# Attention inside a four-block transformer kernel: a shorter lead of the score tiles, and v copied and biased elsewhere

## The reference, cut to what matters

```python
# attention 0 (causal; H = 16 heads of 16)
q, k, v = x @ Wq[h] + bq[h], x @ Wk[h] + bk[h], x @ Wv[h] + bv[h]
probs = softmax(q @ k.T * 16**-0.5 + causal)       # 1024 x 1024 for each head
y = concat_heads(probs @ v) @ Wo + bo
# attention 1: no biases, no mask, q and k turned by rotary tables
```

## Time and profile before

| | |
|---|---|
| median of 3 runs | 689.41 us (688.97 to 691.52) |
| the profiled execution | 690.84 us, its span 689.1 us |
| PE, DVE, ACT, POOL busy | 590.9, 519.1, 349.9, 168.9 us |
| mean granted TensorE clock | 0.901 of 2.4 GHz |
| attention 0: first transposed piece, last row of exponentials | 44.95, 166.17 us |
| attention 1: first transposed piece, last row of exponentials | 370.57, 540.02 us |

### The profile page before, as it was taken

One profiled execution on the slowest core, in us unless ns is written; L12 is line 12 of the kernel. 1 busy time (PEld: TensorE's weight loads), 2 busy tenths in 40 slices (PEclk: granted clock), 3 DMA queues, 4 the chain that ended last, 5 costly groups with the idle time before them and its releaser, 6 DMA issues. The chain is left out here.

```text
span 689.1 us, 12664 instructions
## 1 busy us (share of the span) xinstructions
PE 590.9 (86%) x4702; PEld 406.7 (59%) x4702; DVE 519.1 (75%) x1041; ACT 349.9 (51%) x670; POOL 168.9 (25%) x280
## 2 busy tenths in 40 slices
PE   3989999988489999966979999999999756988793
PEld 2745555545368888855844444444444544778793
DVE  4788888975647777775768899999995587798536
ACT  3226777763145333331223788888888424154451
POOL 4234555563013222130500011111111000014520
PEclk9959999998779999997975999999999955899997
DMA  4534555622231111001340244344332225033431
GB/s 163 67 87 68 88 84 86 93 60 47 54 114 47 46 46 46 23 2 61 42 51 2 39 64 62 50 68 58 55 58 62 50 95 177 1 135 99 150 77 61
DMA packets 27541, 47.15 MB, mean 68 GB/s; under 512 B 13232, under 2 KB 18464, under 8 KB 26208
## 3 DMA queue, kind: packets, MB, share of 16 engines
q1 hardware_dynamic: 22112, 39.11, 27.9%
q0 software_dynamic: 4288, 7.20, 3.8%
q10 hardware_dynamic: 1088, 0.13, 0.1%
HBM read 25.22 MB, written 7.83 MB: 48 GB/s over the span
## 5 line engine op out<-in xcount | busy, mean ns | idle before, releaser
L467 ACT ACTIVATE probs<-ps 128x512 f32<-128x512 f32 x448 | 213.3, 562 | 82.7 <-PE ps L384 82.2
L360 PE MATMUL ps<-k_stack,q_stack 62*128 62x512 f32 x448 | 175.0, 468 | 7.4 <-DVE row_max L563 3.3
L384 PE MATMUL ps<-q_stack,k_stack 64*128 64x512 f32 x448 | 161.8, 439 | 9.6 <-ACT probs L467 5.9
L563 DVE TENSOR_REDUCE row_max<-ps 128x1 f32<-128x1024 f32 x128 | 149.8, 1215 | 17.3 <-PE ps L360 17.3
L384 PEld LDWEIGHTS ps<-q_stack,k_stack 64*128 64x128 f32 x448 | 77.2, 192 | 82.9 <-ACT probs L467 64.1
L399 PE MATMUL ps<-probs,v_ones 128*32 128x256 f32 (+7 forms) x2048 | 118.9, 350 | 4.3 <-POOL probs L518 3.6
L360 PEld LDWEIGHTS ps<-k_stack,q_stack 62*128 62x128 f32 x448 | 80.3, 200 | 37.6 <-DVE row_max L563 16.5
L560 DVE CUSTOM_DVE_ANT_0 y_sums<-ps,wide_mask 128x1024 f32<-128x1024 f32 (+7 forms) x128 | 91.4, 755 | 13.1 <-PE ps L360 11.9
L399 PEld LDWEIGHTS ps<-probs,v_ones 128*32 128x32 f32 x2048 | 52.1, 111 | 48.3 <-issue 16.8
L518 POOL TENSOR_SCALAR_AFFINE_SELECT probs<-probs 128x128 f32<-128x128 f32 x128 | 40.5, 321 | 50.1 <-ACT probs L467 48.4
L874 POOL TENSOR_TENSOR w_chunk_l_m<-y_sums,w_chunk_h_m 128x512 fp32r<-128x512 f32 (+1 forms) x24 | 24.2, 1029 | 99.6 <-ACT w_chunk_h_m L932 92.3
(11 more groups left out here) (203 smaller groups left out, 1115.4 us busy)
## 6 DMA issues: line engine op xcount, KB each, us to landing
y_sums<-in_w_experts SPq DMA_DIRECT2D x8, 1024.0 KB, 4.9
y_sums<-in_w_chunks SPq DMA_DIRECT2D x12, 384.0 KB, 3.0
q_stack<-part_rows SPq DMA_DIRECT2D x32, 128.0 KB, 3.4
k_stack<-part_rows SPq DMA_DIRECT2D x32, 128.0 KB, 3.9
head_sums<-sums POOLq DMA_DIRECT2D x28, 128.0 KB, 2.0
q_stack<-part_rows SPq DMA_DIRECT2D x32, 64.0 KB, 4.0
k_stack<-part_rows SPq DMA_DIRECT2D x32, 64.0 KB, 4.0
q_stack<-max_rows SPq DMA_DIRECT2D x128, 2.0 KB
```

The costliest lines, as they stand in the source:

```text
L360: mm = pe.matmul(scores_bank(s, a, b), stack("q_stack", h, slice(0, TOP))[:, qt * P:(qt + 1) * P], stack("k_stack", h, slice(0, TOP))[:, a ...
L384: pe.matmul(bank(at % 3, 0, b - a), stack("k_stack", h, slice(0, SIDE))[:, kt * P:(kt + 1) * P], stack("q_stack", h, slice(0, SIDE))[:, a: ...
L467: act.activation(probs[:, t % 4, a:b], bank(at % 3, 0, b - a), ACT.Exp).then_inc(exp_done, 1)
L563: dve.tensor_reduce(row_max[:, h % 2, qt:qt + 1], scores_bank(s, 0, end), AX.X, ALU.max).then_inc(scores_free, 1)
```

## The change

The number of score tiles ahead of the loop, 2 x NT = 16, becomes `LEAD = 13`, in both attentions. `EARLY_V` becomes (5, 0): five v projections (attention 0) or none (attention 1) come before the first score tile, and the others one by one behind the first three or eight score tiles. The wait for all 8 units in front of the score tiles becomes a wait for 7 at the first and 8 at the second. ACT copies v in both layers; attention 0's bias is no longer added to v, but in `split`, where the divided heads are cut in two parts. Its memory shrinks from 256 columns, broadcast to all partitions, to 4.

```diff
-EARLY_V = (8, 8)
+EARLY_V = (5, 0)
+LEAD = 13
-            pe.wait_ge(unit_out, 8)
-            for s in range(2 * NT):
+            for s in range(LEAD):
+                if s < 2:
+                    pe.wait_ge(unit_out, s + 7)
                 scores(s, 0)
                 scores(s, 1)
-                if s % 2 and s // 2 + EARLY_V[layer] < NT:
-                    project_v(s // 2 + EARLY_V[layer])
+                if s + EARLY_V[layer] < NT:
+                    project_v(s + EARLY_V[layer])
             pe.wait_ge(v_out, NT)
             for t in range(H * NT):
                 for n in range(2):
                     transposed_scores(t, n)
-                    if t + 2 * NT < H * NT:
-                        scores(t + 2 * NT, n)
+                    if t + LEAD < H * NT:
+                        scores(t + LEAD, n)
                     elif causal:
-                        idle_scores(t + 2 * NT, n)
+                        idle_scores(t + LEAD, n)
...
-            if rope:
-                for tile in range(NT):
-                    act.wait_ge(v_ready, tile + 1)
-                    act.activation(v_ones[:, :, tile, 0:HD], bank(tile % 2, 0, D).rearrange("p (h d) -> p h d", d=HD), ACT.Copy).then_inc(v_out, 1)
+            def v_to_sbuf(tile):
+                act.wait_ge(v_ready, tile + 1)
+                act.activation(v_ones[:, :, tile, 0:HD], bank(tile % 2, 0, D).rearrange("p (h d) -> p h d", d=HD), ACT.Copy).then_inc(v_out, 1)
++            for tile in range(EARLY_V[layer]):
+                v_to_sbuf(tile)
+            for s in range(LEAD):
+                if s + EARLY_V[layer] < NT:
+                    v_to_sbuf(s + EARLY_V[layer])
...
+            def split(high, low, src, bias, high_done, count, low_done):
+                if rope:
+                    dve.tensor_copy(high, src).then_inc(high_done, 1)
+                    dve.wait_ge(high_done, count)
+                    dve.tensor_tensor(low, src, high.bitcast(F32), ALU.subtract).then_inc(low_done, 1)
+                else:
+                    dve.tensor_scalar(high, src, bias, None, ALU.add).then_inc(high_done, 1)
+                    dve.wait_ge(high_done, count)
+                    dve.scalar_tensor_tensor(out=low, in0=src, scalar=bias, in1=high.bitcast(F32), op0=ALU.add, op1=ALU.subtract
+                                             ).then_inc(low_done, 1)
```

More of the change, by code:

```diff
@@ L99, in _ @@
             sp.dma_start(mem["bias_qk"][:, :], dram["bias_qk"]).then_inc(rest_in, 16)
-            sp.dma_start(mem["bias_v"][:, :], dram["bias_v"].broadcast_to([P, D])).then_inc(rest_in, 16)
+            sp.dma_start(mem["bias_v"][:, :], dram["bias_v"]).then_inc(rest_in, 16)
             sp.dma_start(mem["bias_o"][:, :], dram["bias_o"].broadcast_to([P, D])).then_inc(rest_in, 16)
@@ L456, in _ @@
                                ).then_inc(high_ready, 1)
-            if rope:
-                for tile in range(NT):
-                    act.wait_ge(v_ready, tile + 1)
-                    act.activation(v_ones[:, :, tile, 0:HD], bank(tile % 2, 0, D).rearrange("p (h d) -> p h d", d=HD),
-                                   ACT.Copy).then_inc(v_out, 1)
+            def v_to_sbuf(tile):
+                act.wait_ge(v_ready, tile + 1)
+                act.activation(v_ones[:, :, tile, 0:HD], bank(tile % 2, 0, D).rearrange("p (h d) -> p h d", d=HD),
+                               ACT.Copy).then_inc(v_out, 1)
+            for tile in range(EARLY_V[layer]):
+                v_to_sbuf(tile)
+            for s in range(LEAD):
+                if s + EARLY_V[layer] < NT:
+                    v_to_sbuf(s + EARLY_V[layer])
             def exps(t):
@@ L547, in unit_to_flat @@
                     dve.tensor_tensor(dst, dst, turned[:, u % 2, :], ALU.add).then_inc(unit_out, 1)
[L549 to L553, removed]
             def tile_max(s):
@@ L589, in _ @@
                     unit_low(u - 1)
-            if not rope:
-                for t in range(EARLY_V[layer]):
-                    v_to_sbuf(t)
             def invert_group(g):
@@ L601, in _ @@
                     tile_max(s)
-                    if not rope and s % 2 and s // 2 + EARLY_V[layer] < NT:
-                        v_to_sbuf(s // 2 + EARLY_V[layer])
                 finish_max(h)
@@ L614, in group @@
                 dve.wait_ge(group_normed, g + 1)
[L615 to L618, removed]
+                split(yt_h[rows, g, :], yt_l[rows, g, :], normed[rows, g, :], mem["bias_v"][rows, g:g + 1], group_high, g + 1, group_low)
+            def split(high, low, src, bias, high_done, count, low_done):
[8 more added lines that the diff above has]
+                                             ).then_inc(low_done, 1)
             def own_head(h, src):
@@ L628, in own_head @@
                 dve.wait_ge(own_step, count + 3)
-                dve.tensor_copy(own_parts[:, n, 0, :], own[:, n, :]).then_inc(own_step, 1)
-                dve.wait_ge(own_step, count + 4)
-                dve.tensor_tensor(own_parts[:, n, 1, :], own[:, n, :], own_parts[:, n, 0, :].bitcast(F32), ALU.subtract).then_inc(own_step, 1)
+                split(own_parts[:, n, 0, :], own_parts[:, n, 1, :], own[:, n, :], mem["bias_v"][:, KD + n:KD + n + 1], own_step, count + 4, own_step)
             group(0, slice(0, P))
@@ L1487, in program @@
                 "bias_qk": sb(heads, "bias_qk", [P, 4]),
-                "bias_v": sb(heads, "bias_v", [P, D]),
+                "bias_v": sb(heads, "bias_v", [P, KD + 2]),
                 "bias_o": sb(heads, "bias_o", [P, D]),
@@ L1556 @@
             wq.T, wq[swap].T, wk.T, wk[swap].T, a["L1_attn_wv"].T, a["L1_attn_wo"].T]
+    own_bias = [np.tile(np.concatenate([a["L0_attn_bv"].reshape(H, HD)[h], np.zeros(HD, np.float32)]), QUADS) for h in (H - 2, H - 1)]
     router0 = np.concatenate([a["L0_ffn_w_router"], a["L0_ffn_gate_w"], np.zeros((1, D), np.float32)]).T
@@ L1565 @@
         "bias_qk": np.concatenate([a["L0_attn_bq"].reshape(KD, P), a["L0_attn_bk"].reshape(KD, P)]).T,
-        "bias_v": a["L0_attn_bv"].reshape(1, D),
+        "bias_v": np.concatenate([a["L0_attn_bv"].reshape(KD, P), own_bias]).T,
         "bias_o": a["L0_attn_bo"].reshape(1, D),
```

## The result

The changed kernel takes 711.7 us (median of 4 runs, 707.95 to 717.51) against 689.2 for the kernel before on the same chip: ratio 1.031, interval 1.027 to 1.035. It is slower, and by far more than the forecast of 694.2 us says; the time lies outside the range (683.5 to 698.5). Its profiled execution took 714.49 us, span 712.7. Where one execution of a kernel took much longer than its others, the ratios leave it out.

A forecast was written before the change was run, and what follows sets the result against it. It took PE's fixed order, with ACT and DVE handing pieces around, as the bound. Attention 0 at +11.2 and attention 1 at -6.4 gave +4.8, so 694.2 us against the median of 689.41; range 683.5 to 698.5.

The forecast's parts named there:

- Attention 0's loop: the large term: Attention 0's heads 1 to 13: PE waits for DVE's large tiles, period 8.14 instead of 7.10 us; +13.4 us.
- Clock: Attention 1's start: the granted clock falls at the loop's start, same three slow cycles as before; 0, or -3.1 us if held.
- Rival A: Attention 0's loop: PE and DVE absorb the mismatch, only 0.29 us of extra columns a head; 684.6 us, chance 0.28.
- Start of attention 1: Ahead of attention 1's loop: v projections hidden behind DVE's maxima, three maxima move into the loop; gain 10.6 us (bounds 8 and 12).
- Attention 1's loop: Even heads' pieces on the same half run one after the other, times_v 0.36 us later; +4.2 us in all.
- the 0.4 named as a sign: Sign that the forecast is right: even heads of attention 1 are 0.4 us longer than odd ones.
- rival B: Attention 1's start: the clock holds through 5 us of thin work, -3.1 us; 691.1 us, chance 0.12.
- Start of attention 0's loop: times_v waits for POOL's masks until 48.3 against 49.70, gain 1.4 us; the rest of head 0 gives it back: -0.1 us.
- End of attention 0: PE's 2.30 us wait for POOL's mask goes, as head 14's maxima and their spreading come later; -2.2 us (bounds -4.5 and 0).
- Bias: At attention 0's end a copy of 0.69 us becomes an addition of a column; +0.1 us (bounds 0 and 0.9).
- rival C: Attention 0's maxima DMAs land as late as the stack loads, each head waits 0.9 us more; +12, 706 us, chance 0.05.
- Rival D: Attention 1: same-half pieces overlap too, so the halves don't matter; -4.2, 690.0 us, chance 0.07.

The follow-up runs named there:

- e6: Lead 16 in both attentions (v part as changed), attention 1's stacks on swapped halves so that every pair of pieces shares one half; 859.97 us, ratio 1.246.
- e12: Lead 16 in both attentions (v part as changed), attention 0's stacks on swapped halves so that every pair of pieces shares one half; 775.6 us, ratio 1.127.
- e2: The changed kernel with the lead put back to 16 in attention 1 only, 13 kept in attention 0; 710.2 us.
- e4: The changed kernel (lead 13 in both), but DVE takes each row maximum over the first 128 keys only, in both attentions; 697.88 us.
- e7: The changed kernel, with PE repeating score pieces in attention 0 (same half, same values) to fill its gaps; 710.1 us, ratio 1.029.
- e11: e10 with 0.2 us of 128-row matmuls added in each head of attention 0; 699.9 us, ratio 1.013.
- e3: The changed kernel with the lead put back to 16 in both attentions, the v part kept; 685.8 us, ratio 0.991 to 0.998 to the kernel before.
- e1: The changed kernel with the lead put back to 16 in attention 0 only, 13 kept in attention 1; 692.2 us.
- e10: Lead 16 in both attentions (v part as changed), with 128-row matmuls added before score tiles 9 to 15 ahead of attention 1's loop; 694.4 us, ratio 1.005.

## Why the prediction was wrong

**How far off.** The profiled executions lie 23.6 us apart, foreseen were 4.8. Of the 18.9 us between, attention 0's loop has 8.7 (22.1 for 13.4), its end 4.2, its start and head 0 0.8, attention 1's loop 4.3 and its start 2.0; the stretches between and behind give 1.1 back.

**What bounds the kernel.** Right: PE's fixed order with ACT and DVE as partners, head by head.

**Attention 0's loop: the term that failed.** The step that failed is "Attention 0's loop: the large term", which added +13.4 us, all of it as a delay by DVE at an unchanged clock; measured are +22.1. Its links came as written, each within 0.25 us, and the wait stands where it was put; 8.38 against 8.14 us is 0.24 a head, 3 us over 13 heads. The sum missed three things. First, the clock, which "Clock" weighed only for attention 1's start. Low clock behind head 0's sums costs 9.7 us over 8.38 a head (127.0 - 14 x 8.38); before, the wait of the earlier trace rows and the fall behind it cost 4.8 (104.9 - 14 x 7.15). That is +4.9, and with 14 x 1.23 = 17.2 it makes the +22.1 of the table. Second, head 0: PE stays at 1.2 GHz until 65 us, not 54, and the stretch to head 0's sums is 3.0 us longer; foreseen was that it gives back 1.3 of 1.4 gained. Third, the mechanism was read from one side. The prediction called the extra columns 0.29 us and let DVE set the rest; with DVE's load away 0.84 of the 1.24 us are still there. The long score tiles meet short transposed pieces in the second half of the head, which is what the count above says; it fits and is not isolated. Rival A (0.29 a head, 684.6 us, chance 0.28) fails for the same reason: its 0.29, for which the prediction gives no working, is a third of what the longer piece of each pair adds by the count.

**What the same half does.** Foreseen as a delay of 0.36 us in even heads, and in attention 1 it is: 0.46. Its larger effect was not in the text at all: in whole loops of pieces in turn on one half the low clock was not raised (e6, e12).

**The single falls of the clock: cause open.** They are not simply the even heads' pieces in turn. At a lead of 13 the changed kernel, e2 and e4 have 17 falls between them in attention 0's loop, 8 of them in odd heads; at 14 both are in odd heads (11 and 13), at 15 there is none. Ahead of the fall in head 3 no score piece had met a transposed piece of its own half for over 9 us. Nor are they the waits for DVE, which are gone in e4. Filling PE's gaps took the six falls to one in e7; the fall in e11 came with no gap to fill. No run here isolates what makes the clock fall.

**Start of attention 1.** Foreseen -10.6, measured -8.6, within the bounds of 8 to 12. The mis-sized link is PE's tile with a projection: 1.56 us, not 1.28. Less the two score pieces (0.23 each) the projection takes 1.10 us, where 0.74 + 0.08 was foreseen: six matmuls 0.12 us apart are 0.72, and the other 0.38 lies at the two turns between pieces of 62 rows and matmuls of 128. At 1.56 six tiles are 1.7 us longer, most of the 2.0 missed. By e3 the v part gives 4.9 us of the 8.6 and the lead 3.8.

**Attention 1's loop.** Foreseen +4.2, measured +8.5. The serial part was right in mechanism (0.46 for 0.42). Missed: PE waits for DVE's maxima, 0.70 us in even heads and 0.27 in odd ones. The long wait comes behind a head's three short closing instructions on DVE, which is the likely reason; e4, which shortens the maxima, takes both waits away. Even heads are longer than odd ones by 0.9 us, not by the 0.4 named as a sign.

**Clock at attention 1's start.** Right: it fell as the loop began,

```profile
384.00:386.00 2.00, 1.46 (x4) 0.86 0.01 2
```

and cost the slow first cycles as before; rival B is out.

**Start of attention 0's loop.** times_v starts at 48.34, on POOL's mask, as worked out (48.3):

```profile
48.34 1.83 PE L400 MATMUL ps<-probs,v_ones 128*32 128x256 f32 x16 [1.32 <-POOL probs L525]
```

**End of attention 0.** PE's 2.30 us wait for POOL is gone, as said, though e1 with a lead of 16 has no such wait either (e3 has 2.00), so that the lead alone isn't shown to be the reason. The gain was not to be seen: the last stretch is 2.1 us longer. DVE's last group starts 5.03 us behind head 14's sums, not 3.85, behind a wait for a DMA, and the residual comes 0.7 us later behind DVE's last division. In e3, at a lead of 16, this stretch takes 17.0 us too (17.3 in the changed kernel), so it isn't the lead that lengthens it. The last group:

```profile
190.12 1.23 DVE L609 TENSOR_TENSOR y_sums<-y_sums 96x1024 f32<-96x1024 f32 x1 [0.93 <-DMA y_sums<-sum_rows]
191.39 0.75 DVE L621 TENSOR_SCALAR part_rows<-y_sums,bias_v 96x1024 fp32r<-96x1024 f32 x1
192.18 1.28 DVE L623 SCALAR_TENSOR_TENSOR part_rows<-y_sums,bias_v,part_rows 96x1024 fp32r<-96x1024 f32 x1
```

**Bias.** 0.75 for 0.69 us of the earlier trace rows, and 1.28 for 1.22 in the pass behind it: +0.1, as taken.

**The maxima's DMAs (rival C).** No piece waits for them in either attention; the 706 us of C were near the time for another reason. **Rival D** is out by the rows of attention 1: pieces on one half don't start together.

## What to carry to other kernels

When a loop pairs work of falling sizes, shift one side of it only by whole periods: count the columns of a period with the longer of each pair, not the sum (a count that fits here, not a rule that was isolated), and check which half each piece is on. When a change makes PE run in turn what ran side by side, or gives it small waits, price the clock as well as the pieces: look for the nearest loop of that form in a trace, and put a chance on it. And run the parts of a change alone: here the small one (v between the score tiles) was a gain that the large one buried, and it made the lead in attention 1 look free.

## What the runs showed of the hardware

- Pieces of 62 or 64 rows on opposite halves start within 0.01 us of each other; on the same half 0.23 to 0.24 us apart for 512 columns at a granted clock of 1.00 (410.70 and on) and 0.43 at 0.50 (e6).
- A loop that began at a granted clock of 0.50, with PE busy without a gap and its score pieces all on one half at a time, stayed at 0.50 (e6, e12); with the pieces on two halves it went back to 1.00 9 us into the loop (e3).
- The clock fell to 0.50 with PE shown busy without a gap (e10, 360.80 us), and inside a loop in which PE waited no longer than 0.35 us at a time (the changed kernel, six times).
- Matmuls of 128 and of 62 rows in turn: 0.43 us apart for 512 columns at a granted clock of 1.00 (e10), against 0.23 for two of 62 rows on one half, and the page of the profile calls PE busy in both.
- A DVE pass that adds a column scalar cost a little more than the copy or the subtraction that it replaced: 0.75 against 0.69 us and 1.28 against 1.22 for 1024 columns.
